# Second attention on one core: weighing with the values standing in TensorE, the weighed heads evicted in fours, and counts and maxima moved around VectorE's branch

## The reference

```
attn = softmax(q @ k.T / sqrt(8))              # 16 heads of 8 dimensions, 256 x 256 scores each
k_keep = max(1, int(256 * (1 - sr)))           # sr = 0.1 + 0.9 * sigmoid(ema - thr), one per head
keep = rank of each score in its row < k_keep
w = where(keep, attn, 0);  w = w / (sum(w) + 1e-10)
out = (w @ v) @ Wo.T + bo
```

## Time and profile before

| | us |
|---|---|
| median of three runs | 2043.77 (2037.28 to 2046.5) |
| the profiled execution | 2043.58, its span 2041.8 |
| second attention, from its first scores to its last sum | 491 to 1109 of the span |
| iterations n = 0 to 7 of its loop, by the starts of `past` | 585.2 to 1069.2, and the last one to 1106 |

### The profile page before, as it was taken

The page is one execution under the profiler, slowest core; times in us unless marked ns, Lnnn a source line. Parts: engine busy times, 40 slices in busy tenths (PEclk is TensorE's granted clock), DMA queues, the critical chain, the costliest instruction groups (busy, mean ns, idle before and its releaser), DMA issues.

```text
span 2041.8 us, 38862 instructions
## 1 busy us (share of the span) xinstructions
PE 1642.0 (80%) x12640; PEld 1172.7 (57%) x12640; DVE 1476.3 (72%) x4747; ACT 1115.7 (55%) x3322; POOL 877.4 (43%) x1162
## 2 busy tenths in 40 slices
PE   3888989897358988988779978527777799999978
PEld 3445667675236766766668645413443477777763
DVE  6678776555588988999887842358876777887657
ACT  2444444445988898899852423214452366666620
POOL 3333221124253554444433577676300377767610
PEclk8889999997555555555557989858896899999969
DMA  4111101003000000000001023322110000000000
GB/s 139 47 47 41 40 21 42 18 2 122 15 9 17 12 13 11 17 9 9 1 1 59 23 78 110 97 65 73 48 72 20 15 1 1 2 1 2 1 1 21
DMA packets 67305, 67.58 MB, mean 33 GB/s; under 512 B 9955, under 2 KB 58966, under 8 KB 66566
## 3 DMA queue, kind: packets, MB, share of 16 engines
q1 hardware_dynamic: 58930, 53.09, 7.9%
q0 software_dynamic: 5120, 10.50, 2.0%
q10 hardware_dynamic: 3040, 1.38, 0.2%
HBM read 30.41 MB, written 8.39 MB: 19 GB/s over the span
## 4 chain that ended last, share of the span: by engine, by line
PE 35%; DVE 27%; ACT 12%; issue 10%; POOL 6%; SPq 6%; ACTq 2%; DMA 1%; DVEq 0%; POOLq 0%
SPq L689 5%; POOL weights L1165 4%; DVE weights L3212 3%; PE bank L2143 3%; PE bank L1551 3%; PE bank L2103 3%; ACT big L4445 3%; PE bank L1567 3%; DVE weights L3156 3%; DVE nmax L3072 2%; DVE small L3200 2%; PE bank L1758 2%; PE bank L2130 2%; ACT rope_s L4235 2%; ACT rope_c L4235 2%
## 5 line engine op out<-in xcount | busy, mean ns | idle before, releaser
L1758 PEld LDWEIGHTS bank<-V,probsT 128*128 128x128 f32 x1024 | 203.6, 297 | 28.4 <-ACT probsT L4246 13.7
L1758 PE MATMUL bank<-V,probsT 128*128 128x9 f32 x1024 | 205.4, 333 | 15.2 <-ACT probsT L4246 10.9
L2711 DVE TENSOR_REDUCE nmax<-bank 128x4 f32<-128x1024 f32 x144 | 175.9, 1221 | 51.8 <-PE bank L1331 48.8
L891 POOL TENSOR_TENSOR big<-big,rinv 128x512 f32<-128x512 f32 x128 | 131.7, 1049 | 45.7 <-DVE rinv L3767 45.7
L1745 PE MATMUL bank<-silu_b,weights 128*128 128x128 bf16 x464 | 138.9, 303 | 0.0
L4050 ACT ACTIVATE feat_o<-bank 128x1024 f32<-128x1024 f32 x72 | 73.7, 1023 | 101.5 <-PE bank L1331 66.7
L4050 ACT ACTIVATE O<-bank 128x1024 f32<-128x1024 f32 x72 | 73.7, 1024 | 97.2 <-PE bank L1331 70.6
L3761 DVE TENSOR_REDUCE nmax<-bank 128x2 f32<-128x512 f32 x128 | 81.9, 682 | 58.1 <-PE bank L2103 58.1
L4445 ACT ACTIVATE big<-bank,nmax 128x256 f32<-128x256 f32 x256 | 117.6, 478 | 11.1 <-DVE nmax L3761 11.1
L4453 ACT ACTIVATE big<-bank 128x512 f32<-128x512 f32 x128 | 73.8, 614 | 68.8 <-PE bank L2130 68.8
L4246 ACT ACTIVATE probsT<-bank 128x512 f32<-128x512 f32 x128 | 75.9, 600 | 58.4 <-PE bank L1745 39.0
(11 more groups left out here) (818 smaller groups left out, 5110.5 us busy)
## 6 DMA issues: line engine op xcount, KB each, us to landing
qT<-parts SPq DMA_DIRECT2D x276, 32.0 KB
big<-V SPq DMA_DIRECT2D x192, 32.0 KB
y_rows<-weights SPq DMA_DIRECT2D x24, 256.0 KB, 2.3
big<-parts SPq DMA_DIRECT2D x180, 32.0 KB
weights<-in_weights_l_ffn SPq DMA_DIRECT2D x1, 4832.0 KB, 14.3
weights<-in_weights_l_attn SPq DMA_DIRECT2D x1, 3904.0 KB, 13.0
qT<-V SPq DMA_DIRECT2D x96, 32.0 KB
weights<-in_weights_l_ffn SPq DMA_DIRECT2D x1, 2860.0 KB, 11.7
```

The lines of the kernel that those rows point to most:

```text
L891: nc.gpsimd.tensor_tensor(row, row, rinv[:, h % H, :].unsqueeze(2).to_broadcast([P, T, S]), ALU.mult).then_inc(scaled.sem, 1)
L1758: last = mm(pb[1][:, t * S + h * wide:t * S + (h + 1) * wide], probsT[:, h % 2, at:at + P], values_of(b, k)[:, h * wide:(h + 1) * wide], s ...
L2711: V_.tensor_reduce(to, scored.rearrange("p (i a n) -> p i a n", i=HPG, n=n), AX.X, ALU.max, negate=True).then_inc(score_max.sem, 1)
```

## The change

Six things, with the diff cut to them:

1. `ROWS_DVE` is 8 in place of 6, in all three counts.
2. The values stand in TensorE (128x9) and the turned probabilities of both query tiles move through (256 columns). Each head takes 2 float32 products in place of 4. Head h writes partitions 32 (h mod 4) and up of the first half of the bank, so four heads fill it.
3. After every fourth head ScalarE evicts the four (`l1_take_quad`), and TensorE turns them back to tokens with two products against the identity (`l1_turn_quad`). Three of the fours land in the second half of the same bank, the last one in its first half.
4. `weighed` on VectorE has two parts for its sums and two for its products.
5. On VectorE `count_below(n + 1, 0)` and `ask_doubt` stand ahead of the maxima, which stand between the copied number and the branch.
6. On TensorE the turning of head 14 moves ahead of the weighing of head 12. The two semaphores `z_psum` and `z_ready` of the fourth feed-forward part are now `side_psum` and `side_taken` with a use in both stages.

```diff
-ROWS_DVE = 6
+ROWS_DVE = 8
+QUADS = H // 4
...
+        weighed_quad = V[:, 0, 576:576 + S]
+        early_heads = 3 * H // 4
+        weighed_at = ((slice(0, early_heads), pb[1][:, S:S + T * early_heads * (HD + 1)]),
+                      (slice(early_heads, H), pb[1][:, 0:T * (H - early_heads) * (HD + 1)]))
...
-                wide = HD + 1
-                for t in range(T):
-                    for k in range(T):
-                        at = t * S + k * P
-                        last = mm(pb[1][:, t * S + h * wide:t * S + (h + 1) * wide], probsT[:, h % 2, at:at + P],
-                                  values_of(b, k)[:, h * wide:(h + 1) * wide], start=k == 0, stop=k == T - 1)
+                wide, part = HD + 1, slice(32 * (h % 4), 32 * (h % 4) + HD + 1)
+                by_keys = probsT[:, h % 2, :].rearrange("p (t k n) -> p k t n", t=T, k=T)
+                for k in range(T):
+                    last = mm(pb[1][part, 0:S].rearrange("p (t n) -> p t n", t=T), values_of(b, k)[:, h * wide:(h + 1) * wide], by_keys[:, k],
+                              start=k == 0, stop=k == T - 1)
                 last.then_inc(pv_done.sem, 1)
+
+            def l1_turn_quad(b, q, ph="l1_attn"):
+                pe.wait_ge(side_taken.sem, side_taken(ph, b, q + 1))
+                of_heads = C("ident").rearrange("p (j d) -> p j d", j=4)[:, :, 0:HD + 1]
+                heads_there, there = weighed_at[q // 3]
+                at = 4 * q - heads_there.start
+                for t in range(T):
+                    o = there.rearrange("p (t h d) -> p t h d", t=T, d=HD + 1)[:, t, at:at + 4, :]
+                    last = mm(o, weighed_quad[:, t * P:(t + 1) * P], of_heads, start=True, stop=True)
+                last.then_inc(side_psum.sem, 1)
...
                     if now(n):
                         l1_doubt(n)
+                    if now(n - 1):
+                        l1_turn_quad(n - 1, QUADS - 1)
...
                     if now(n):
+                        l1_turn_quad(n, 0)
                         l1_weigh(n, 4)
...
                         l1_weigh(n, 7)
                         l1_turn_probs(n, 9)
                         l1_turn_probs(n, 10)
+                        l1_turn_quad(n, 1)
                         l1_weigh(n, 8)
...
                         l1_turn_probs(n, 13)
                         l1_weigh(n, 11)
+                        l1_turn_probs(n, 14)
+                        l1_turn_quad(n, 2)
                         l1_weigh(n, 12)
-                        l1_turn_probs(n, 14)
                         l1_turn_probs(n, 15)
...
+                l1_turn_quad(B - 1, QUADS - 1)
                 l1_turn_out(B - 1)
...
-                dve.wait_ge(pv_done.sem, pv_done(ph, b, H))
+                dve.wait_ge(side_psum.sem, side_psum(ph, b, QUADS))
...
+                for of, there in weighed_at:
+                    o1 = there.rearrange("p (t h d) -> p t h d", t=T, d=HD + 1)
+                    link(V_.scalar_tensor_tensor(kept_sum[:, :, of], sums_by_tile[:, :, of], 1e-10, o1[:, :, :, HD], ALU.mult, ALU.add))
...
                 for n in range(-1, B):
+                    if now(n + 1):
+                        count_below(n + 1, 0)
                     if now(n):
+                        ask_doubt(n)
                         largest_of(n, 0)
                         largest_of(n, 1)
-                        ask_doubt(n)
                         settle_doubt(n)
...
                     if now(n + 1):
-                        count_below(n + 1, 0)
                         first_move(n + 1)
...
+            def l1_take_quad(b, q, ph="l1_attn"):
+                act.wait_ge(pv_done.sem, pv_done(ph, b, 4 * q + 4))
+                nc.scalar.activation(weighed_quad, pb[1][:, 0:S], ACT.Copy).then_inc(side_taken.sem, 1)
...
                     if now(n):
+                        l1_take_quad(n, 0)
                         l1_take_probs(n, 5)
...
                         l1_take_probs(n, 8)
+                        l1_take_quad(n, 1)
                     if now(n + 1):
                         l1_count(n + 1, 2, 25, ROWS1)
...
                     if now(n + 2):
                         l1_exps(n + 2, 13)
+                    if now(n):
+                        l1_take_quad(n, 2)
+                    if now(n + 2):
                         l1_start(n + 2)
                         l1_count(n + 2, 0, ROWS_DVE, 10)
...
                         l1_exps(n + 2, 15)
+                    if now(n):
+                        l1_take_quad(n, QUADS - 1)
+                    if now(n + 2):
                         l1_count(n + 2, 0, 17, 20)
```

More of the change, by code:

```diff
@@ L606, in adaln_program @@
         ranks_psum = wide_signal("ranks_psum", l1_ffn=3, l2_ffn=2 * PAIRS)
-        z_psum = signal("z_psum", l2_ffn=1)
-        z_ready = signal("z_ready", l2_ffn=1)
+        side_psum = signal("side_psum", l1_attn=QUADS, l2_ffn=1)
+        side_taken = signal("side_taken", l1_attn=QUADS, l2_ffn=1)
         rope_ready = signal("rope_ready", l3_attn=2 * NQ3)
@@ L1753, in l1_weigh @@
                 pe.wait_ge(probsT_ready.sem, probsT_ready(ph, b, h + 1))
-                wide = HD + 1
-                for t in range(T):
-                    for k in range(T):
-                        at = t * S + k * P
-                        last = mm(pb[1][:, t * S + h * wide:t * S + (h + 1) * wide], probsT[:, h % 2, at:at + P],
-                                  values_of(b, k)[:, h * wide:(h + 1) * wide], start=k == 0, stop=k == T - 1)
-                last.then_inc(pv_done.sem, 1)
+                wide, part = HD + 1, slice(32 * (h % 4), 32 * (h % 4) + HD + 1)
[3 more added lines that the diff above has]
+                              start=k == 0, stop=k == T - 1)
+                last.then_inc(pv_done.sem, 1)
+            def l1_turn_quad(b, q, ph="l1_attn"):
[3 more added lines that the diff above has]
+                at = 4 * q - heads_there.start
+                for t in range(T):
+                    o = there.rearrange("p (t h d) -> p t h d", t=T, d=HD + 1)[:, t, at:at + 4, :]
+                    last = mm(o, weighed_quad[:, t * P:(t + 1) * P], of_heads, start=True, stop=True)
+                last.then_inc(side_psum.sem, 1)
             def l1_doubt(b, ph="l1_attn"):
@@ L2059, in l2_fall @@
                     last = mm(pb[6][:], W(ph, "win2")[:, c * P:(c + 1) * P], gelus(c), start=c == 0, stop=c == O2 - 1)
-                last.then_inc(z_psum.sem, 1)
+                last.then_inc(side_psum.sem, 1)
             def l2_out(p, ph="l2_ffn"):
                 pe.wait_ge(pass_done.sem, pass_done(ph, p, 1))
-                pe.wait_ge(z_ready.sem, z_ready(ph, p, 1))
+                pe.wait_ge(side_taken.sem, side_taken(ph, p, 1))
                 for j in range(2 * T):
@@ L3225, in weighed @@
                 linkup()
-                V_.tensor_tensor(tokens1.rearrange("p t (h d) -> p t h d", h=H), o1[:, :, :, 0:HD],
-                                 kept_sum.unsqueeze(3).to_broadcast([P, T, H, HD]), ALU.mult).then_inc(tok_ready.sem, 1)
+                for of, there in weighed_at:
+                    o1 = there.rearrange("p (t h d) -> p t h d", t=T, d=HD + 1)
+                    heads_there = of.stop - of.start
+                    last = V_.tensor_tensor(tokens1.rearrange("p t (h d) -> p t h d", h=H)[:, :, of], o1[:, :, :, 0:HD],
+                                            kept_sum[:, :, of].unsqueeze(3).to_broadcast([P, T, heads_there, HD]), ALU.mult)
+                    if of.stop == H:
+                        last.then_inc(tok_ready.sem, 1)
+                    else:
+                        link(last)
             def l1_result(b, ph="l1_attn"):
@@ L4424, in l2_ffn @@
             def l2_ffn(p, ph="l2_ffn"):
-                act.wait_ge(z_psum.sem, z_psum(ph, p, 0))
+                act.wait_ge(side_psum.sem, side_psum(ph, p, 0))
                 for c in range(O2):
```

7 lines of the change are left out of this document (2 added, 5 removed).

## The result

The changed kernel takes 2035.8 us, median of 20 executions (2028.3 to 2043.5), beside 2047.6 us for the kernel before, median of 20 (2037.3 to 2061.1): a ratio of 0.993, 95% interval 0.991 to 0.995. It is 0.7% faster; forecast were 2057.5 us and slower.

A forecast was written before the change was run, and what follows sets the result against it. VectorE's program plus the seam was taken to set the period. Five iterations at +2.7 us (+13.5), then +0.9, -1.7, +2.3 and -1.1, gave +13.9 on 2043.6: 2057.5 us, range 2032 to 2066.

The forecast's parts named there:

- the last iteration: Iteration n = 7: turnings, last eviction and `weighed`, less a saving for heads side by side, make it 2.3 us longer.
- The second eviction: ScalarE's eviction waits for head 7 and blocks count 2's last seven rows; VectorE waits 1.7 us in `settle_on`, five iterations.
- The fourth eviction: ScalarE's eviction after the last weighing delays its count 0 rows, so VectorE waits about 1.0 us at `first_move` each iteration.
- TensorE's tail: At the seam, delayed scores and turnings push head 15 some 0.5 us behind VectorE's counts: +0.1 us an iteration.
- the branch: VectorE's branch before `past`, with the maxima now ahead of it, costs +0.4 us, one MAX8 leaving the queue.
- `weighed`: On VectorE, one small sum and one product more: +0.3 us an iteration, bounds 0.2 and 0.6.
- The seam: VectorE around `past`: count 0's eight rows fill the wait, six rows leave from behind `past`, -2.4 us; the branch +0.4.
- rival C: The branch waits for the maxima: +2.3 us more in seven iterations, 2073 us; chance 0.08.
- rival A: TensorE goes to 2.4 GHz in the stage and neither ScalarE wait arises: 2035.8 us; chance 0.20.
- The two rows: Two more rows on VectorE cost 0.80 us a count; counts 1 and 2 together +1.6 us an iteration.
- The lead-in: Iteration n = -1: VectorE +0.8 us in its first count, ScalarE, the bound there, -1.9 us: -1.1 us.
- the working for the weighing: TensorE's new four-matmul head takes 1.71 us at 1.2 GHz as before; only 0.7 us comes off, at the seam.

The follow-up runs named there:

- e5: The changed kernel again, unaltered, on one chip with later runs: 2032.6 us, ratio 0.990 to the kernel before.
- e4: The changed kernel with six rows on VectorE in place of eight: 2035.7 us, ratio 0.989 to the kernel before.
- e1: The kernel before with VectorE's new order alone, six rows and the old weighing kept: 2051.6 us, ratio 0.998.
- e2: The whole change except the weighing: new VectorE order and eight rows, old weighing, against the kernel before: 2044.6 us, ratio 0.995.
- e9: The changed kernel, but batches 0 to 6 use the old weighing and only the last the new: 2038.7 us, ratio 0.994 to the kernel before.
- e11: e7's kernel run once more later: 2030.9 us, ratio 0.990 to the kernel before.
- e6: The changed kernel with five of ScalarE's last seven rows of count 2 ahead of the second eviction: 2031.4 us, ratio 0.989 to the kernel before.
- e3: The kernel before with the new weighing, evictions and turnings alone, old order and six rows: 2042.3 us, ratio 0.993.
- e7: e6 with seven rows on VectorE in place of eight: 2030.9 us, ratio 0.989 to the kernel before.
- e8: e2 with eight unread bf16 matmuls added on TensorE ahead of each head's weighing: 2077.3 us, ratio 1.010 to the kernel before.
- e10: e9 with seven rows on VectorE: 2034.1 us, ratio 0.992 to the kernel before.
- e16: e2's kernel again, one more execution profiled: 2057.3 us.

## Why the prediction was wrong

Forecast were 13.9 us more; the medians say 11.8 less. For the seven periods I had +12.7 us and they measure -8.5; for the last iteration +2.3, and it measures -6.6 in the mean of the profiles. The steps that failed are four terms. The second eviction's wait (+8.5) took TensorE to be at 1.2 GHz in every one of five iterations, and cost 1.5. The fourth eviction's wait (+6.0) took both of its chains to start together, and there is none. TensorE's tail (+0.1 each) kept the doubt product late, and its wait fell by 5.1. The last iteration was priced from one profile. Two small terms, the branch and `weighed`, were too dear by 1 to 1.5 us each in the stage.

**The seam (-2.4, +0.4).** Right in sign, low in what it gains. Count 0 is 3.20 us between the end of `doubt` and the copied number; the doubt product, which cost 0.97 us in iteration 3, was no longer late. From the number to `past` are 4.15 to 4.45 us in seven of the eight seams, against 3.89 to 4.39: I took +0.4, it was about +0.2. The maxima do run beside the branch; rival C is refuted. The Trainium skill, Advanced Engine Details and Errata, section Engine Queue Depths, gives VectorE a queue of eight, and the seam agrees with it: all eight maxima, 2.71 us of them, stood ahead of the branch and `past` came 4.15 us behind the number, as before.

**The second eviction (+1.7 in five iterations), the step that the forecast called decisive.** The mechanism is there; the forecast had the clock of its chain wrong in most iterations. ScalarE waits for head 7, and VectorE then waits for ScalarE. The changed kernel in iteration n = 2, TensorE, then ScalarE, then VectorE:

```profile
758.19 0.70 PE L1705 MATMUL bank<-kT,probs 128*128 128x256 f32 x2 [2.30 <-DVE probs L3059]
758.72 0.78 PE L1707 MATMUL bank<-probs,kT 128*128 128x16 f32 x4
759.43 1.88 PE L1762 MATMUL bank<-probsT,V 128*9 128x256 f32 x4
```

```profile
761.35 0.38 ACT L4278 ACTIVATE V<-bank 128x256 f32<-128x256 f32 x1 [2.65 <-PE bank L1762]
```

```profile
765.24 0.19 DVE L3125 TENSOR_TENSOR small<-small,routes 128x32 f32<-128x32 f32 x1 [0.87 <-ACTq L4267]
```

From gram's end to the counts are 7.1 us here, not 7.85: spread took 1.24 us in place of 1.78, since the clock changed within the stretch. Where head 7 is weighed at 2.4 GHz (1.03 us, in n = 1, 3 and 4), VectorE doesn't wait at all. That point, 6.1 us against 6.15, was worked out rightly under rival A. In n = 0 and 2 head 7 takes 1.88 us and the waits are 0.62 and 0.87. The second profile of the changed kernel (e5) has one iteration, n = 1, in which spread and head 7 both run at 1.2 GHz (1.82 and 1.88 us). There ScalarE waits 3.17 us, from gram's end to the counts are 7.7 us, and VectorE waits 1.44:

```profile
689.59 0.38 ACT L4278 ACTIVATE V<-bank 128x256 f32<-128x256 f32 x1 [3.17 <-PE bank L1762]
```

```profile
693.48 0.19 DVE L3125 TENSOR_TENSOR small<-small,routes 128x32 f32<-128x32 f32 x1 [1.44 <-ACTq L4267]
```

That is nearly the forecast's chain of 7.85 and its wait of 1.7. So the chain was right for the low clock, and the step that failed is the clock: the whole term is 1.5 us in the first profile and 2.0 in e5, not 8.5. That the clock keeps this wait away is its part in the periods. (In the working for the weighing, 634 and 379 ns differ by 255 ns and not 213; the 0.43 us that it led to was measured.)

**The fourth eviction (+1.0 in six iterations).** ScalarE's own chain was right: from head 15's end at 787.22 to its last row at 795.9 are 8.7 us, forecast 8.8. What failed is where VectorE stands against it. I had head 15 end behind VectorE's counts, so that both chains start together. It ended 2.3 us ahead of the copied number (787.22, 789.48), with TensorE no longer late. With six rows the wait is there, 1.0 us each (e4); with eight it is not. No run has the evictions at the low clock throughout, so how much of this is the clock's stays open. And e1 shows the other side of the same wait: I had priced the order by VectorE's rows alone and never asked what it costs without the two rows that ScalarE gives up.

**The small terms.** TensorE's tail, +0.1 an iteration, was of the other sign: the waits for the doubt product went from 5.4 to 0.3 us in seven. They are 0.3 in e2 too, at 0.55, so VectorE's longer counts hide the product, and not the clock. `weighed` takes 1.07 us up to the next start in place of 0.94 (805.20 to 806.14 in the kernel before), +0.1 where I had +0.3. The two rows were right: VectorE's busy time rose by 12.7 us in seven periods, 1.8 each, and count 0's share of it lies in the seam. The lead-in's -1.1 can't be told: the first `past` comes at 578.4 to 585.2 us in the five profiles of the kernel before, and VectorE has some 5 us more to do ahead of it, with count 0 of batch 1 there.

**The last iteration (+2.3), the largest miss.** I took it from one profile, 40.0 us at a grant of 0.71, and added turnings. It is the one place where TensorE is the bound, and with the old weighing it takes 38 to 57 us; the profile I had was among the better ones. The new weighing holds 0.90 or 0.91 there and takes 37.7 to 38.5 us in every profile but that of e9 and e11 (39.5 us at 0.89, 39.1 at 0.85). The five profiles of before have 40.0, 45.2, 38.2, 49.1 and 49.1, in the mean 44.3, so this term is -6.6 on average (-2.2 against the profile that I had). The rows that should have warned me were my own: grants of 0.87 and 0.51 within that iteration.

**The sum again**, by the means of the profiles (five of before, two of the changed kernel): periods 67.95 against 69.17 in seven, -8.5; last iteration -6.6; up to the first `past` +1.0 (582.4 against 581.4); behind the stage, where the change does nothing, +1.4 (936.0 against 934.6 us). -12.7 in all, beside -11.8 by the medians.

**Rival A** named the right time, 2035.8, by luck, and half the right reason. It took 7.8 us from a baseline of 2043.6; the measured change is 11.8 from 2047.6. The clock did rise, and it did keep the evictions' wait small. But most of what A has the clock pay for came without it: e2 shows the periods at 0.55 just as short. The Trainium skill, TensorE: Matmul & The Clock Gate, section What's actually happening, has it that activity releases the clock. The rows here don't bear it out as busy time: 416 busy us of 484 stand beside 0.54, and 334 of 476 beside 0.81. Which part of the new weighing lifts the clock stays open.

## What to carry to other kernels

Before a sum rests on one profile, look for the stretch in which TensorE is the bound and ask what its clock does there in other executions; a change that steadies it is worth the mean of those, not the best. An order that fills a wait pays only if the engines that feed the next waits have slack, so price the reorder together with the shift of work, and each alone. Where a new wait is worked out as one chain against another, write down from which event both start, since that was wrong for the fourth eviction here, and not the durations. And before two periods are compared, look in each seam for a longer branch: here one, 2.3 us longer than the rest, came and went with edits made for other reasons.

## What was not expected of the hardware

Every seam of the two kernels has a fetch of instructions about 2.2 us (1.9 to 2.4) behind the copied number, and `past` starts about 2.0 us after it. In one seam of the changed kernel, the fifth, `past` comes 6.56 us behind the number, and there are two fetches. The DMA queues in that seam, after the branch (40 slices of 0.1625 us; the fetches stand in slices 12 and 27, at about 861.1 and 863.5):

```profile
GB/s 0 0 0 0 0 0 0 0 0 0 0 0 50 0 0 0 0 0 0 0 0 0 0 0 0 0 0 50 0 0 0 0 0 0 0 0 0 0 0 0
q14 instruction: 2, 0.02, 0.8%
```

```profile
865.54 0.42 DVE L3212 TENSOR_TENSOR weights<-const,small 128x256 f32<-128x256 f32 x1 [3.56 <-issue]
```

It is the same seam in the second profile of the changed kernel (6.61 us) and in e6 (6.41), and in the kernel before the second seam in all five (6.3 to 6.5 us), as in e3 (6.15), so it goes with the program, not with the execution. In e2, e4, e7 to e11 and e16 no seam has it; e1 has one of 6.57 us, and e1 and e4 one of about 5 each. It is worth some 2.3 us to each comparison of periods between a kernel that has it and one that hasn't; before against changed it cancels. That the 4.15 us of each branch are mostly this fetch is argued from the times and was not tried; the Trainium skill, Runtime: NRT & Kernel Launch, section Instruction fetch mechanics, says that a taken branch to a page not at hand has to fetch it first, and the rows agree: `past` follows the last fetch by 1.9 to 2.3 us in both kernels.

The new weighing's four matmuls of a head take 1.03 us at 2.4 GHz and 1.88 at 1.2 GHz, 0.25 and 0.43 to 0.47 us from one to the next; heads in different quarters of the bank did not run side by side, for which I had taken off 0.7 us.
